# Gate and up products of the later dense chunks in three parts of the rounded type

## The reference

```python
x = x + 0.5 * ffn(layernorm(x))          # (16, 256, 128), f32
x = x + attn(layernorm(x))               # 16 heads of 64, causal softmax over 256
x = x + 0.5 * ffn(layernorm(x))          # same weights as the first

def ffn(h):                              # 4096 tokens of width 128, 64 experts of width 64
    tidx, tw = gate(h)                   # sigmoid scores, best 4 of 8 groups, best 8 experts
    y = sum over experts e: tw[:, e] * ((silu(h @ We_gate[e]) * (h @ We_up[e])) @ We_down[e])
    return y + silu(h @ Ws_gate) * (h @ Ws_up) @ Ws_down
```

## Time and profile before

| | |
|---|---|
| median of 3 runs | 1599.59 us (1598.91 to 1600.77) |
| the profiled execution | 1599.95 us |
| its span, first to last instruction | 1598.2 us |
| granted TensorE clock, mean | 0.988 |
| PE busy | 1525.0 us, 95% |
| DVE busy | 1166.0 us, 73% |
| ACT busy | 766.1 us, 48% |
| POOL busy | 715.0 us, 45% |

### The profile page before, as it was taken

One profiled execution on the slowest core, in us unless ns is written; L12 is line 12 of the kernel. 1 busy time (PEld: TensorE's weight loads), 2 busy tenths in 40 slices (PEclk: granted clock), 3 DMA queues, 4 the chain that ended last, 5 costly groups with the idle time before them and its releaser, 6 DMA issues. The chain is left out here.

```text
span 1598.2 us, 27345 instructions
## 1 busy us (share of the span) xinstructions
PE 1525.0 (95%) x8683; PEld 969.3 (61%) x8683; DVE 1166.0 (73%) x3354; ACT 766.1 (48%) x2105; POOL 715.0 (45%) x1093
## 2 busy tenths in 40 slices
PE   5899999999899899999999999999999999999998
PEld 2344444444788677777777776776438884444443
DVE  4698888765354578899898988764796845668675
ACT  2234323222455577777777776775325552232222
POOL 1000088888222234333333204665831226878730
PEclk9999999999999899999999999999999999999999
DMA  9999655563587101000000000112646884666552
GB/s 186 217 255 248 158 127 139 130 147 93 156 225 219 56 24 26 23 23 25 23 25 23 18 2 31 49 49 70 162 107 172 228 222 112 147 143 150 134 131 66
DMA packets 202043, 181.31 MB, mean 113 GB/s; under 512 B 39408, under 2 KB 154288, under 8 KB 201904
## 3 DMA queue, kind: packets, MB, share of 16 engines
q1 hardware_dynamic: 175056, 132.34, 35.2%
q0 software_dynamic: 16384, 33.59, 7.7%
q10 hardware_dynamic: 10464, 13.63, 2.5%
HBM read 121.83 MB, written 57.67 MB: 112 GB/s over the span
## 5 line engine op out<-in xcount | busy, mean ns | idle before, releaser
L868 ACT ACTIVATE f_hid<-banks 128x512 f32<-128x512 f32 (+1 forms) x264 | 157.6, 597 | 507.4 <-PE banks L828 507.3
L488 POOL DMA_INDIRECT x_rows<-r_xk,r_idx x256 | 262.8, 1026 | 125.8 <-issue 51.7
L890 DVE TENSOR_TENSOR f_hid<-banks,f_hid 128x512 f32<-128x512 f32 (+1 forms) x264 | 181.7, 688 | 144.2 <-ACT f_hid L868 144.0
L840 PE MATMUL banks<-f_hid,wd 128*128 128x512 f32 x528 | 272.7, 600 | 10.6 <-DVE f_hid L903 10.6
L824 PE MATMUL banks<-r_xT_d,gu 128*128 128x512 f32 x528 | 276.5, 606 | 4.2 <-DMA wd<-in_L_ffn_We_down 2.6
L828 PE MATMUL banks<-r_xT_d,gu 128*128 128x512 f32 x528 | 272.5, 598 | 0.0
L524 POOL DMA_INDIRECT a_g<-y_rows,r_idx x128 | 126.8, 990 | 237.3 <-ACT a_probT L1386 93.1
L903 DVE TENSOR_TENSOR f_hid<-f_mix_wide,f_hid 128x512 f32<-128x512 f32 x256 | 176.0, 688 | 30.3 <-DMA f_mix_wide<-mix_rows 27.9
L840 PEld LDWEIGHTS banks<-f_hid,wd 128*128 128x128 f32 x528 | 99.3, 191 | 143.4 <-issue 119.5
L828 PEld LDWEIGHTS banks<-r_xT_d,gu 128*128 128x128 f32 x528 | 101.0, 191 | 130.2 <-issue 126.4
L824 PEld LDWEIGHTS banks<-r_xT_d,gu 128*128 128x128 f32 x528 | 97.2, 192 | 119.5 <-issue 109.9
(11 more groups left out here) (243 smaller groups left out, 2875.7 us busy)
## 6 DMA issues: line engine op xcount, KB each, us to landing
f_mix_wide<-mix_rows SPq DMA_DIRECT2D x124, 512.0 KB
x_rows<-zero ACTq DMA_DIRECT2D x12, 1024.0 KB, 6.4
f1q_xq<-x_rows SPq DMA_DIRECT2D x48, 256.0 KB, 3.2
y_rows<-f1q_yq SPq DMA_DIRECT2D x48, 256.0 KB, 2.4
f2q_xq<-x_rows SPq DMA_DIRECT2D x48, 256.0 KB, 3.3
y_rows<-f2q_yq SPq DMA_DIRECT2D x48, 256.0 KB, 2.5
x_rows<-r_xk,r_idx POOLq DMA_INDIRECT x256
wd<-in_L_ffn_We_down SPq DMA_DIRECT2D x7, 512.0 KB, 10.8
```

What stands on the lines that cost most here:

```text
L488: nc.gpsimd.indirect_dma_start(x_rows[:, :], bass.IndirectOffsetOnAxis(ap=b.idx[:, f, CT * k + t, j:j + 1], axis=0), b.xk[:, k, t, :], Non ...
L840: mm = nc.tensor.matmul(acc[:, :], w["wd"][0:rows, 2 * p, :], d.hid[0:rows, g % HIDS, :], start=(p == 0), stop=(p == PAIRS))
L868: nc.scalar.activation(d.hid[0:rows, g % HIDS, :], gate_bank[g % 3][0:rows, :], ACT.Silu)\
L890: nc.vector.tensor_tensor(d.hid[0:rows, g % HIDS, :], up_bank[g % 3][0:rows, :], d.hid[0:rows, g % HIDS, :], ALU.mult).then_inc(gated, 1)
```

## The change

In chunks behind the first of a run of dense chunks (chunks 1 to 3 of `ffn_first`, chunks 2 and 3 of `ffn_second`: 99 and 66 slots), each gate and each up product becomes three products of type f32r that accumulate in one bank. The weights are split while the chunk before goes by: in slot g ScalarE writes the rounded part `gu_high` of the pair of slot g - 4, and VectorE the rest `gu_low` (256 elements in each partition, 33 times a stage). The chunk's tokens are split likewise (`x_high`, `x_low`, 512 elements, once a chunk). In the last dense chunk of `ffn_first` VectorE puts the weights together again (`weights_back`, 33 times), since `gu_high`'s room is given to the attention weights and the quads read `gu`; the quads' first gate and up products wait for that. The attention weights are now loaded between quads 6, 9 and 12 of SyncE's list, and split in halves in quad steps 20 to 35; half of the `weigh` steps (36 to 67) move from slots 98 to 129 into the quad steps 0 to 31. In `ffn_second` `gu_high` takes the room of the quad buffers, so that the first split waits for the quads' last stores.

```diff
+SPLIT_LAG = 4
...
 def up(g):
...
+            if c > two.chunk:
+                if p == 0:
+                    pe.wait_ge(x_low_done, x_parts(c))
+                if c == two.chunk + 1:
+                    pe.wait_ge(w_low, p + 1)
+                xh, xl = two.xh[:, c % 2, :], b.xT_low[:, c % 2, :]
+            for kind, bank in enumerate((gate_bank, up_bank)):
+                if kind == 1 and g >= 3:
+                    pe.wait_ge(gated, g - 2)
+                o = bank[g % 3][0:rows, :]
+                plain = w["gu"][:, kind, experts, :].rearrange("p e f -> p (e f)")
+                if c <= two.chunk:
+                    mm = nc.tensor.matmul(o, plain, x, start=True, stop=True)
+                else:
+                    high, low = (m[:, kind, experts, :].rearrange("p e f -> p (e f)") for m in (two.high, w["gu_low"]))
+                    nc.tensor.matmul(o, low, xh, start=True, stop=False)
+                    nc.tensor.matmul(o, high, xh, start=False, stop=False)
+                    mm = nc.tensor.matmul(o, high, xl, start=False, stop=True)
+            mm.then_inc(pair_done, 1)
...
+        def weights_high(p):
+            if p == 0:
+                for s, v in two.free:
+                    act.wait_ge(s, v)
+            act.wait_ge(pair_done, SLOTS * two.chunk + p + 1)
+            nc.scalar.copy(both(two.high, p), both(w["gu"], p)).then_inc(w_high, 1)
...
+        def weights_low(p):
+            dve.wait_ge(w_high, p + 1)
+            nc.vector.tensor_tensor(both(w["gu_low"], p), both(w["gu"], p), both(two.high, p).bitcast(F32),
+                                    ALU.subtract).then_inc(w_low, 1)
+
+        def weights_back(p):
+            dve.wait_ge(silu_done, SLOTS * two.back + p + 1)
+            dve.wait_ge(gated, SLOTS * two.back + p + 1)
+            nc.vector.tensor_tensor(both(w["gu"], p), both(two.high, p).bitcast(F32),
+                                    both(w["gu_low"], p).bitcast(F32), ALU.add).then_inc(w_low, 1)
+
+        def x_low(c):
+            dve.wait_ge(x_high_done, x_parts(c))
+            dve.wait_ge(r.logits_done, routes[c].front + 1)
+            nc.vector.tensor_tensor(b.xT_low[:, c % 2, :], d.xT[:, c % 2, :], two.xh[:, c % 2, :].bitcast(F32),
+                                    ALU.subtract).then_inc(x_low_done, 1)
...
-SPLIT_AT = {70: (0,), 74: (1,), 78: (2,)}
+SPLIT_AT = {20 + 3 * n: (n,) for n in range(6)}
+LOAD_AT = {6: 0, 9: 1, 12: 2}
+WEIGHED = 36
...
-        if 0 <= at < WEIGH_STEPS:
+        if 0 <= at < WEIGH_STEPS and at + WEIGH_STEPS * k < WEIGHED:
...
+            two = two_parts(room, nc, "f1_", 0, {10: 1, 54: 2, 83: 3}, 3)
...
+        qd = quads(ctx, nc, "f1q_", w, x_all, psum, b, q, x_rows, y_rows, r, chunk_of, whole=(dn.w_low, 2 * SLOTS))
...
             for j in range(QUAD_STEPS):
                 quad(j)
...
+                for i in SPLIT_AT.get(j, ()):
+                    weight_low(i)
+                for i in range(WEIGHED + j, min(WEIGHED + j + 1, SPARSE * WEIGH_STEPS)):
+                    weigh(*divmod(i, WEIGH_STEPS))
...
-                    elif c == 1 and n < 3:
-                        load_attention(n)
             sp.wait_ge(dn.x_updated, DENSE)
             for i in range(QUADS_R + STORE_LAG):
                 quad(i)
+                if i in LOAD_AT:
+                    load_attention(LOAD_AT[i])
...
+        two = two_parts(ctx, nc, "f2_", 1, {SLOTS + 10: 2, SECOND_AT[7] + T_LOGITS + 2: 3})
...
+        two.free = [(qd.y_stored[side], 16 * len(range(side, QUADS_R, YBUFS))) for side in range(YBUFS)]
```

More of the change, by code:

```diff
@@ L600, in gate_up @@
             e = expert[j]
+            if j == 0 and whole is not None:
+                pe.wait_ge(*whole)
             pe.wait_ge(xT_copied, j + 1)
@@ L786, in dense_buffers, with two_parts, dense @@
     return d
-def dense(ctx, nc, tag, w, x_all, gate_bank, up_bank, acc, misc, d, mix_rows, r, routes, ready=None, split=None, before_banks=()):
+def two_parts(ctx, nc, tag, chunk, x_at, back=None):
+    two = Parts()
+    two.high = ctx.enter_context(nc.sbuf_tensor(tag + "gu_high", [P, 2, E + 1, F], F32R))
+    two.xh = ctx.enter_context(nc.sbuf_tensor(tag + "x_high", [P, 2, CHUNK], F32R))
+    two.chunk, two.x_at, two.back, two.free = chunk, x_at, back, ()
+    return two
+def dense(ctx, nc, tag, w, x_all, gate_bank, up_bank, acc, misc, d, b, mix_rows, r, routes, two, ready=None, split=None, before_banks=()):
     def sem(name):
@@ L798, in dense, with weights_at, both, x_parts @@
     first_spread = sem("first_spread")
+    w_high, w_low, x_high_done, x_low_done = (sem(n) for n in ("w_high", "w_low", "x_high_done", "x_low_done"))
     NS = SLOTS * len(routes)
+    def weights_at(g, chunk):
+        p = g - SLOTS * chunk - SPLIT_LAG
+        return p if 0 <= p < SLOTS else None
+    def both(t, p):
+        return t[:, :, 2 * p:min(2 * p + 2, E + 1), :]
+    def x_parts(c):
+        return c - two.chunk
     def parts(g, drain):
@@ L882, in slot @@
                 silu(g)
+                p = weights_at(g, two.chunk)
+                if p is not None:
+                    weights_high(p)
+                if g in two.x_at:
+                    x_high(two.x_at[g])
         return slot
@@ L917, in slot @@
                 weighted_product(g)
+                p = weights_at(g, two.chunk)
+                if p is not None:
+                    weights_low(p)
+                if g in two.x_at:
+                    x_low(two.x_at[g])
+                if two.back is not None and g // SLOTS == two.back:
+                    weights_back(g % SLOTS)
             if update:
```

100 lines of the change are left out of this document (52 added, 48 removed).

## The result

| | before | changed |
|---|---|---|
| median of 4 runs each, us | 1600.18 (1598.91 to 1601.82) | 1588.47 (1587.16 to 1588.98) |
| span of the profiled execution, us | 1598.2 | 1587.3 |

The ratio is 0.9925, with a 95% interval of 0.991 to 0.9939: 12 us faster, not the 25 of the forecast. The time lies outside the forecast's own range (1567 to 1583 us) and inside the wide one (1560 to 1590 us), near its slow end.

A forecast was written before the change was run, and what follows sets the result against it. TensorE bounds the dense chunks; places and 204 us of scatters bound `ffn_first`. 1599.95 less 25.5 (`ffn_second`), less 1 (first scatter), plus 1.5 (quads) gives 1575 us; own range 1567 to 1583, wide range 1560 to 1590.

The forecast's parts named there:

- What bounds: Dense chunks bound by TensorE, 2.57 us a slot; `ffn_first` by places, 204 us of scatters, 5.5 us for landing and load.
- The product's price: Dense slots: an f32r product of 512 columns costs 0.22 us (0.2145 to 0.236), so a slot takes 2.18 us, 0.395 less.
- 131 ns for a stream with weight loads: Rival, `ffn_second`: products at 131 ns, VectorE's 1.9 us bounds the slot, 44 us saved there, 1557 us; chance 0.01.
- VectorE in FFN2's slots 66 to 83: `ffn_second`, heavy slots 73 to 82: VectorE falls 3 to 4 us behind, three banks hold that; 0.5 us lost, up to 4.
- The signs that the prediction named for being wrong: `ffn_second`'s slot stays above 2.4 us, or `ffn_first` ends more than 8 us from where it does now.
- First scatter: `ffn_first`: the first scatter starts 1 us earlier than 197.2 us; bounds 4 us earlier and 6 us later.
- Scatters: `ffn_first`: the 128 scatters stay 204 us, 5 us either way; `weights_back` lengthening and the dense chunks' earlier end net zero.
- TensorE's wait for the table: `ffn_first`: dense chunks end near 358 us, four quads by 370, then TensorE waits 25 to 40 us for first table rows.
- Quads of FFN1: `ffn_first`'s quads carry 1.5 MB more of loads; the backlog costs 1.5 us, bounds 0 to 5.
- the gain taken in `ffn_second`: Rival: late landings or uneven VectorE work keep slots near 2.35 us, 14.5 us saved, 1586 us; chance 0.17 including late scatter.

The follow-up runs named there:

- the changed kernel's second profile: The changed kernel itself run once more with nothing altered, on another chip; ratio 0.9927 (0.9912 to 0.9943) to the kernel before.

## Why the prediction was right and wrong

**What bounds: right.** The slots of dense chunks are bound by TensorE, FFN1 by the places of the rows and the scatters. The forecast that FFN1's saving mostly turns into waiting is what the runs with one stage alone and with fewer scatters show.

**The product's price: mis-sized.** Taken at 0.22 us; it is 0.230, near the upper bound of 0.236 that 256 columns give in proportion. The argument that the surplus over a bare pass "should not double" was wrong: it nearly does, the price goes by columns (2 x 0.1161 = 0.232). That costs 66 slots x (0.395 - 0.326) = 4.6 us. The Trainium skill (TensorE: Matmul & The Clock Gate, Back-to-back issue gap) would have 0.216 us, which these rows don't bear out; its 131 ns for a stream with weight loads they bear out still less.

**VectorE in FFN2's slots 66 to 83: the step that failed.** It was given 0.5 us, with 4 as a bound, because three banks could hold a lag of 3 to 4 us. The banks hold most of it: the down products wait 2.4 us for hidden values. But the turns of tokens and of mixing rows wait for VectorE's own work or for the one bank that all turns share, not for one of the three, and stand in TensorE's order in front of the next products: 3.3 and 1.5 us, for 1.5 and 0.7 before. The clock of 0.74 behind the longest wait is 2.6 us more, and the prediction had no term for that. Slots 66 to 83 were to be about 6.2 us shorter and became 2.8 us longer; without the price's part (1.2 us) that is 7.8 us. 5.6 us of it come back when the turns stand later (from slot 65 to the end, 170.3 us in the changed kernel's second profile and 164.7 with the later turns). The wait was visible before, at 1.53 us; I had not asked which waits would grow as TensorE gets faster. The signs that the prediction named for being wrong (a slot above 2.4 us, or FFN1's end 8 us from where it was) both stayed away, so they couldn't have shown this.

**First scatter: right within the bounds, not in its sign.** The forecast was 1 us earlier than 197.22, with bounds of 4 earlier and 6 later. It is at 197.5 to 202.1 us in twelve profiles, 198.8 in the middle; without splits it is at 197.22 to 199.07. The 202.12 of the first profile misled me into a theory about the splits, which fell.

**Scatters: right within the bounds.** Forecast 204 us, 5 either way; 198.3 to 200.0 us from the first to the last start in eight profiles (203.4 before, 203.8 with FFN1's chunks as before, 200.5 with three parts in two chunks). The difference lies in the last dense chunk, where one starts each 1.52 us with three parts and each 1.65 us without. So the additions of `weights_back` beside them don't lengthen the scatters on balance; why they are quicker wasn't tried.

**TensorE's wait for the table: wrong in size.** The prediction called it its main claim. Forecast 25 to 40 us, measured 14.4 to 14.8 (12.8 once). The dense chunks end at 380 to 384, not at 358. Slot 58 begins at 192 to 197 us for the 192 I put, the slots are 0.07 us longer (5 us), and beyond quiet slots 58 to 130 lose 19 us where I had put 5 and the kernel before loses 9. In that TensorE waits 9.3 us for VectorE between 200 and 300 us, 6.0 of it at turns, with clocks of 0.92 (213 to 233 us) and 0.91 (273 to 293 us): the same step that failed in FFN2. It costs nothing here, since the scatters end later, and so didn't spoil the sum.

**Quads of FFN1: about right.** +1.5 forecast with 0 to 5 as bounds, +2.1 measured, at the same clock over their first 10 us (0.74, and 0.73 before). With the loads there but no three parts it was +0.9 at a clock of 0.83, which is worth another 1 us. TensorE waits only 0.4 us for a table load in them.

**Not foreseen.** Attention, +1.8 us: I took code that isn't touched to be without cost, and the change moves its buffers. The gift of 1.6 us in FFN2's chunk 1 is for the most part a clock of 0.84 where the kernel before's one profile had 0.72; 0.4 us at equal clock stay open.

The sum: of 25 us, 4.6 went to the price, 7.8 to the waits and the clock behind them, 1.8 to places, 1.7 to a clock that fell by chance; chunk 1 gave 1.6 back, mostly by chance too. That leaves 10.7, where the two profiled spans differ by 10.9. The time is near the case "the gain taken in `ffn_second`", given 0.17, though by waits at turns and the price, not by spreads or the total of VectorE's work. The fault in the chances was to price VectorE's lag only against buffers.

## What to carry to other kernels

When the bound engine is made faster, list the places where it waits for another engine in program order, even if they are short today: each grows by the lead that is won, and may take clock with it. Moving such steps a few slots later brought 9.8 us here, nearly what the cheaper products had brought (11.7 us). And when a change moves allocations, compare the rows of untouched instructions before looking for causes in the schedule.

## What the hardware showed

- Products of f32r with 256 columns start 0.1161 or 0.1195 us apart by the places of their operands in SBUF; the records of the f32 products with `po` last 383 or 378 ns. Products of f32r with 512 columns cost 0.230 us, at two places of x.
- TensorE's granted clock behind a wait of 3.3 us (4.9 in one of them) was 0.70 to 0.85 over the next 10 us in all six profiles looked at that have this wait, and behind one of 2.8 us 0.83 or 1.00, without difference in that stretch of the program (lower in ten of twelve profiles). 1.00 is the 2.4 GHz level, and 0.5 would be 1.2 GHz throughout.
- Scatters without a spacer (1.26 us apart), or with one of half the width (1.35), hold up the queue of the spreads, so that TensorE stands for up to 29 and 22.5 us at a time: 5.2% and 2.35% of the kernel's time. At 1.46 us apart it doesn't.
- One profile is not enough for a start: the same FFN1 had its first scatter between 197.47 and 202.12 us.
